# A wait for the landing of the preceding pair in front of every second indirect DMA of a mixture-of-experts stage

## The reference

```python
shared = jnp.einsum('bth,hd->btd', jax.nn.silu(jnp.einsum('btd,dh->bth', x, sw1)) * jnp.einsum('btd,dh->bth', x, sw2), sw3)
probs = jax.nn.softmax(jnp.einsum('btd,de->bte', x, rw) + rb, axis=-1)
w, idx = jax.lax.top_k(probs, TOP_K)
w = w / jnp.sum(w, axis=-1, keepdims=True)
gates = jnp.sum(w[..., None] * jax.nn.one_hot(idx, N_EXPERTS, dtype=x.dtype), axis=-2)
h = jax.nn.silu(jnp.einsum('btd,edh->beth', x, ew1)) * jnp.einsum('btd,edh->beth', x, ew2)
eout = jnp.einsum('beth,ehd->betd', h, ew3)
routed = jnp.einsum('betd,bte->btd', eout, gates)
return shared + routed
```

## Time and profile before

| what | value |
|---|---|
| time, median of 3 runs | 1792.38 us (1787.33 to 1798.26) |
| span of the profiled execution | 1895.4 us |
| PE, DVE, ACT, POOL busy in it | 1386.3, 1268.0, 845.2, 881.2 us |
| L2009, indirect DMAs of the experts | 80 per mixture, 76.7 and 76.9 us busy |
| L1550, indirect DMAs of the routing | 16, 48 and 64 |
| mean granted TensorE clock | 0.854 |

### The profile page before, as it was taken

One profiled execution on the slowest core, in us unless ns is written; L12 is line 12 of the kernel. 1 busy time (PEld: TensorE's weight loads), 2 busy tenths in 40 slices (PEclk: granted clock), 3 DMA queues, 4 the chain that ended last, 5 costly groups with the idle time before them and its releaser, 6 DMA issues. The chain is left out here.

```text
span 1895.4 us, 27842 instructions
## 1 busy us (share of the span) xinstructions
PE 1386.3 (73%) x8207; PEld 690.9 (36%) x8208; DVE 1268.0 (67%) x2981; ACT 845.2 (45%) x1215; POOL 881.2 (46%) x775
## 2 busy tenths in 40 slices
PE   4359999999999888766885776775865445546882
PEld 1113333333333555445773221321311003335772
DVE  4666999999983576643332498999989995533333
ACT  3404666666667332213442776484573321112441
POOL 3401121121212645753554169788696664652552
PEclk9756999999999899878997887886986666878996
DMA  4721111211120331622224578959758636114225
GB/s 131 238 79 41 54 53 44 62 47 52 57 64 16 101 103 47 180 65 80 78 72 121 156 164 207 231 131 246 181 156 215 162 99 165 62 62 121 79 75 150
DMA packets 218312, 210.68 MB, mean 111 GB/s; under 512 B 49247, under 2 KB 188482, under 8 KB 215874
## 3 DMA queue, kind: packets, MB, share of 16 engines
q1 hardware_dynamic: 196174, 180.70, 35.8%
q0 software_dynamic: 9216, 19.02, 3.1%
q10 hardware_dynamic: 12800, 9.46, 1.6%
HBM read 145.27 MB, written 63.37 MB: 110 GB/s over the span
## 5 line engine op out<-in xcount | busy, mean ns | idle before, releaser
L804 ACT ACTIVATE attn_prob<-attn_ps_cols 128x1024 f32<-128x1024 f32 (+1 forms) x320 | 292.1, 940 | 219.5 <-PE attn_ps_cols L680 218.5
L2534 POOL TENSOR_TENSOR ssm_hc<-ssm_h,ssm_cb 128x1024 f32<-128x1024 f32 x128 | 300.6, 2356 | 135.2 <-DVE ssm_h L2517 111.1
L2517 DVE TENSOR_TENSOR_SCAN ssm_h<-ssm_decay,ssm_ps_u 128x1024 f32<-128x1024 f32 x128 | 292.7, 2286 | 29.9 <-ACT ssm_decay L2505 13.7
L830 POOL TENSOR_SCALAR_AFFINE_SELECT attn_prob<-attn_prob 128x512 f32<-128x512 f32 x128 | 81.2, 634 | 415.7 <-ACT attn_prob L804 415.7
L712 DVE CUSTOM_DVE_ANT_0 attn_ps_rows<-attn_ps_rows,const_mask_rows 128x384 f32<-128x384 f32 (+3 forms) x512 | 236.0, 520 | 39.7 <-PE attn_ps_rows L647 37.5
L647 PE MATMUL attn_ps_rows<-attn_ks,attn_qs 72*128 72x512 bf16 (+3 forms) x768 | 228.4, 351 | 44.4 <-DMA attn_qs<-parts_dram 31.2
L2505 ACT ACTIVATE ssm_decay<-ssm_wide,ssm_aneg 128x1024 f32<-128x1024 f32 x128 | 146.1, 1146 | 174.4 <-DVE ssm_h L2517 96.3
L2468 PE MATMUL ssm_ps_u<-ssm_stack,ssm_spread 96*128 96x512 bf16 x256 | 95.9, 465 | 155.3 <-DVE ssm_h L2517 148.5
L680 PE MATMUL attn_ps_cols<-attn_qs,attn_ks 75*128 75x512 bf16 (+3 forms) x768 | 194.3, 333 | 4.7 <-DMA attn_qs<-attn_nrows 4.1
L699 PE MATMUL attn_ps_o<-attn_prob,attn_vw 128*32 128x512 f32 (+3 forms) x1536 | 166.6, 506 | 0.3 <-POOL attn_prob L830 0.3
L717 DVE TENSOR_REDUCE attn_nm<-attn_ps_rows 128x1 f32<-128x512 f32 x256 | 157.8, 681 | 7.8 <-PE attn_ps_rows L647 7.7
(11 more groups left out here) (361 smaller groups left out, 2491.9 us busy)
## 6 DMA issues: line engine op xcount, KB each, us to landing
ssm_wide<-delta_dram SPq DMA_DIRECT2D x128, 512.0 KB, 6.7
attn_ks<-parts_dram SPq DMA_DIRECT2D x48, 192.0 KB
attn_qs<-parts_dram SPq DMA_DIRECT2D x48, 192.0 KB
parts_dram<-proj_parts SPq DMA_DIRECT2D x8, 768.0 KB, 3.8
ffn1e_x<-ex_dram SPq DMA_DIRECT2D x40, 130.0 KB
ffn2e_x<-ex_dram SPq DMA_DIRECT2D x40, 130.0 KB
split_dram<-ssm_parts SPq DMA_DIRECT2D x6, 768.0 KB, 4.4
ssm_stack<-split_dram SPq DMA_DIRECT2D x18, 256.0 KB, 4.3
```

What stands on the lines that cost most here:

```text
L804: nc.scalar.activation(prob[u % RING][:, heads[0]:heads[-1] + 1, 0:w], ps_cols[s % 2][:].rearrange("p b (x q) -> p (b x) q", x=len(heads) ...
L2517: nc.vector.tensor_tensor_scan(h[t % H_RING][:], decay[t % DECAY_RING][:], ps_u[t % 2][:], 0.0, ALU.mult, ALU.add).then_inc(scan_done, 1)
L2534: nc.gpsimd.tensor_tensor(hc[:, t % HC_RING, :], h[t % H_RING][:], cb[b % 2][:], ALU.mult).then_inc(hc_done, 1)
```

## The change

A constant `PACED = 2` is added. In `scatter`, for every even DMA of a unit (the first, third, fifth and seventh of eight) POOL waits until all DMAs issued before it have landed, which are those of the same unit or, for the first, of the preceding unit; the very first has no wait. In `run_experts` POOL waits, ahead of a tile's first indirect DMA, until both of the preceding tile have landed. So at most two scatters are under way at any time. Nothing else is changed.

```diff
--- before.py
+++ after.py
@@ -1328,6 +1328,7 @@
 PADROW = TOP * N
 AHEAD = 8
 OUTS = 8
+PACED = 2
 UNITS_IN = N // UNIT
 DEEP = 8
 GROUP_ENDS = [1, 3, 5, UNITS_IN]
@@ -1545,6 +1546,11 @@
         pool.wait_ge(r.id_ready, u + 1)
         pool.wait_ge(r.gate_ready, u + 1)
         pool.wait_ge(r.pos_ready, u + 1)
+        pool.sem_inc(r.passed, 1)
+    before = u * TOP * UPT + j - 1
+    if before >= 0 and j % PACED == 0:
+        v, at = before // (TOP * UPT), before % (TOP * UPT)
+        pool.wait_ge(r.sent[v % DEEP], (v // DEEP * TOP * UPT + at + 1) * 16)
         pool.sem_inc(r.passed, 1)
     n, j = j // UPT, j % UPT
     nc.gpsimd.indirect_dma_start(dram["ex"], bass.IndirectOffsetOnAxis(ap=r.pos[k][:, n, j:j + 1], axis=0),
@@ -2005,6 +2011,9 @@
                     s = i * AHEAD + q
                     for j in range(SUB):
                         pool.wait_ge(out_ready, now(s * SUB + (j + 1)))
+                        if j == 0 and past(s, 1):
+                            ui, uq = shifted(i, q, -1)
+                            pool.wait_ge(sent[uq], now(ui * (SUB * 16) + SUB * 16))
                         pool.sem_inc(passed, 1)
                         nc.gpsimd.indirect_dma_start(dram["ey"], bass.IndirectOffsetOnAxis(ap=x[q][:, j, TOKEN:TOKEN + 1].bitcast(I32), axis=0),
                                                      out[q % OUTS][:, j, :], None).then_inc(sent[q], 16)
```

## The result

The changed kernel takes 2042.84 us (median of 4 runs, 2038.9 to 2048.35), the kernel before, on the same chip, 1795.32 us (1787.33 to 1801.57). The ratio is 1.139, 95% interval [1.135, 1.144]: 247.5 us slower. The forecast was 1981 us with a range up to 2015, so the direction was right, 188 us of the rise were foreseen, and the time lies 28 us above the range.

What follows compares the result with a forecast made beforehand. No engine was full; unprofiled experts ran at PE's 2.84 us a tile, routing at POOL's scatter burst. Pairs of 4.15 us add 34.7 + 46.9 + 51.1 + 51.1 + 4.7 = 188 to 1792.4: 1981 us, range 1895 to 2015.

Steps and rivals of the forecast that it cites:

- routing 1: First routing stage's scatters: 23 pairs at 4.15 us make 96.7 us against a floor of 62, so +34.7 us.
- routing 2: Second routing stage's scatters: 31 pairs at 4.15 us make 129.9 us against a floor of 83, so +46.9 us.
- experts 1: First experts stage's scatters: 39 pairs at 4.15 us make 163.1 us against a floor of 112, so +51.1 us.
- experts 2: Second experts stage's scatters: 39 pairs at 4.15 us make 163.1 us against a floor of 112, so +51.1 us.
- memory stage and opening: Early scatters: 3.3 us for two waits at routing 1's opening, 1.4 us in the memory stage, together 4.7 us.
- the floors: Stretch lengths without held completions: 62 and 83 us in routing, 112 us in each experts stage.
- the waits on "remote": Unexplained ACT and DVE waits in experts and routing: completions held, 76 us too long, mostly only in the profiled execution.
- the landing of 2.1 us: Time from a pair's second scatter's start to its landing, all stages; with 0.79 and 1.26 us, a 4.15 us pair.
- rival 1: Routing and experts: holds occur in every execution, so the sum is 112 us, 1904 us in all; chance 0.20.
- 2 (PE cools, 2040 us): Experts: slower pairs lower PE's clock, a tile doubles to 5.7 us; half priced, about 2040 us; chance 0.05.
- 3: All paced scatters: waits already met, landing and wake-up hidden, 2.52 us a pair, 1792 us; chance 0.04.
- 4: Routing and experts: holds are real, pacing ends them, pairs take at most 2.84 us; 66 us faster, 1726 us; chance 0.05.

Runs made afterwards that it cites:

- the runs with 68, 140 and 284 waits: Kernel before plus a wait ahead of every fourth scatter, every second (the change itself), and every scatter: 1908.2, 2042.84 and 2314.1 us.
- the plain stores: Kernel before with the experts' indirect scatters replaced by one plain SP store per tile, no wait added: 1790.7 us, ratio 0.996.

## Why the prediction was wrong in size, point by point

The table sets its terms beside the difference of after's stretches to those of the kernel before as profiled again.

| term | forecast, us | measured, us |
|---|---|---|
| routing 1 | 34.7 | 105.9 - 62.3 = 43.6 |
| routing 2 | 46.9 | 147.9 - 84.0 = 63.9 |
| experts 1 | 51.1 | 170.4 - 111.5 = 58.9 |
| experts 2 | 51.1 | 173.8 - 111.5 = 62.3 |
| memory stage and opening | 4.7 | 71.3 - 54.7 = 16.6 |
| sum | 188 | 245.3 (spans: 245.7) |

**What bounds the kernel, and the floors: right.** The step that looked boldest, to sum against floors that the trace did not show, is borne out to 1 us a stretch. The gap between span and median had to have a cause, and most of it was the waits on "remote". The reason given, something that holds completions "while POOL scatters", went too far: POOL scatters in the same way in the two other profiles of that kernel, and nothing is held. Of the section of the Trainium skill that the prediction weighed (NOTIFIC — the notification-queue block, Overflow: three behaviours, one of which stalls the engine), no run here shows more than this: if trace records stalled the engines, they did so in one profile of three of the same kernel. The holds also took more than the 76 us: the steps from routing's last scatter to the experts' first were 24.2 and 31.3 us, and are 15.8 and 16.1 us in the kernel as profiled again, 24 us more, which makes the whole gap of 100. So the span of after could not keep the 30 us above the time that the prediction left it: with that execution gone, all of the gap went.

**The mechanism: right.** POOL waits for a DMA in front of each pair, the 4.1 to 4.3 us foreseen for a pair are 4.28 in the experts, and the runs with 68, 140 and 284 waits put 1.65 to 1.83 us on each.

**The failing step is the landing of 2.1 us**, taken from one refill of SP in the experts and used as a constant for all stages. The 2.72 us that it calls a bound come from one scatter at the quiet end of a stage, and bound nothing elsewhere. It failed twice.
- In rest it is 2.2 to 2.3 us. The pair then takes 4.28 us in the experts and 4.35 in routing, not 4.15: 78 x 0.13 + 54 x 0.20 = 21 us of the 57 that are missing.
- Elsewhere it is longer, the longest cases beside bulk transfers, and that is the rest, 36 us. The opening makes 11.9 of these, with three waits of 4.8 to 6.5 us; the third, in front of routing 1's own first scatter, the sum had not counted at all. In the stretches it is 24: steady circles would give 101.3, 136.1, 168.2 and 168.2 us, and they last 4.6, 11.8, 2.2 and 5.6 us longer. In routing 2 the largest part is one wait. In after SP's store of the zeros stands just ahead of it, and SP began to issue the experts' loads 10.7 us ahead of the stage's first scatter:

```profile
1677.37 0.38 SPq L1669 DMA_DIRECT2D ex_dram<-ffn2r_zeros  x1
...
1687.15 0.96 POOL L1556 DMA_INDIRECT ex_dram<-ffn2r_xn,ffn2r_pos  x1 [7.91 <-issue]
```

The kernel with the loads moved tells the two apart (SP's and POOL's timeline):

```profile
1679.94 0.38 SPq L1664 DMA_DIRECT2D ex_dram<-ffn2r_zeros  x1
...
1688.63 0.96 POOL L1556 DMA_INDIRECT ex_dram<-ffn2r_xn,ffn2r_pos  x1 [2.84 <-issue]
```

The store still goes out there, and the same wait is 2.84 us; two pairs of 9.25 and 7.18 us come in the middle of the stage instead, where the loads went. So this wait hung on the loads, alone or together with the store behind them. For the other late landings of the stretches (pairs up to 1.5 us longer, and once 4.1, at the start of the second experts stage) no run tells what they wait for. In after, from 1775 us on, SP's stores over, every pair of that stage takes 4.33 to 4.46 us.

The estimate of 2.15 us by the Trainium skill (DMA: Bandwidth & Descriptors, Anatomy of one DMA) is 0.1 us short of the view's 2.2 to 2.3; that section's constant fixed part holds for a scatter by itself, and the view's maximum of 7.7 us shows what it leaves out.

The late landings were there before too: the kernel before has landings up to 7.6 us (above), but nobody waited for them. The prediction saw SP's queue only in the experts, and asked of SP who waits for POOL, not what of SP's POOL would now wait for.

**The range** stopped at a landing halfway to its bound. Its own sum there gave 2020 us, and it ended at 2015 without a reason. At the full bound of 2.72 us the same sum gives 132 x 0.62 = 82 us more, 2063 us, which would have held the time, though by luck: the landings were not late by 0.6 us each, but most by 0.1 to 0.2 and a few by up to 6. Its low end was spent on rival 1.

**The rivals.** 1 (holds in every execution, 1904 us) fell by the two other profiles, and by the plain stores for the holds of the experts. 2 (PE cools, 2040 us) gives nearly the measured time by another mechanism: the clock did fall, but POOL kept the pace (ACT's evictions, and so PE's matmuls ahead of them, were done 2 to 21 us before it needed them), and the missing us are found elsewhere. 3 and 4 fell: in the four stretches no wait is met, and a pair takes over 4 us.

## What to carry to other kernels

A wait for one's own DMA makes a circle of wake-up, burst and landing. Once that is the slowest circle of the stage, each wait costs it less the step without the wait, whoever set that step (here POOL's 2.52 us in routing, PE's 2.84 in the experts); one step further back (tried in the experts, two pairs) it was free. Price a landing in every stage where the wait will stand, and look there for bulk transfers of other queues: landings that are late in a stage where nobody waits for them show in no stall before. When the span of a profile lies well outside the timed runs (here 5.7% above their median), profile the same kernel again before reading stalls from it.

## What the runs showed of the hardware

- One profiled execution of three of the same kernel was 100 us longer (1895.4 against 1794.8 and 1790.2 us), by waits that end on nothing the trace names.
- An indirect scatter of 128 rows lands 2.2 to 2.3 us after it starts, behind four in a row as behind two (3.01 us from the last start to the next, 3.04 with pairs). The view's longest is 7.7 us; two of the longest waits for a landing, 6.46 and 7.91 us, fell to 3.03 and 2.84 when SP's loads of 0.5 and 1 MB ahead of them were moved, and 7.54 us turned up where the loads went.
- 76 waits that were met when POOL came to them cost nothing that could be measured: ratio 1.001 [0.998, 1.004].
